# An out projection that keeps its weights standing, ten pair additions, a new order of steps, and VectorE filling a PSUM bank itself

## The chip, the cores and the metric

The kernel runs as one program on one core of a Trainium2 chip. The metric is the device time of one execution in microseconds, the median of several runs. TensorE multiplies, VectorE and ScalarE do elementwise work and can reach PSUM, GpSimd (POOL) does elementwise work in SBUF only, and SyncE (SP) issues most of the DMAs. Each engine goes through its own queue in order and waits on semaphores.

## What is computed

For 32 sequences of 128 tokens with 128 features each, in fp32:

```python
h = adapter_with_layernorm(x, language_ids)          # per-sequence weights
for layer in range(4):                               # mamba blocks
    xz = layer_norm(h) @ Wi.T;  xs, z = split(xz)
    u = silu(causal_conv4(xs) + cb)                  # 256 channels
    dt, B, C = split(u @ Wx.T);  dt = softplus(dt @ Wdt.T + bdt)
    # for each of 16 states: s = exp(dt*A)*s + dt*B*u ;  y += s*C
    y = (y + u*Dp) * silu(z)
    h = h + y @ Wo.T
x = x + h
x = x + sparse_moe(dense_moe(x))                     # dense: 8 experts and a shared one
```

The recurrence over tokens is done with one scan instruction for each pair of states.

## The kernel before

After a setup phase (the adapter) comes the **wave phase** (`wave_phase`), then a dense phase and a sparse phase for the experts. The change is in the wave phase alone.

The wave phase has NIT = 32 iterations; an iteration is one layer of one group of G = 4 sequences (512 tokens, TOK). The groups are taken in two rounds of four. An iteration `i` has NSTEP = 16 steps `k`: steps 0 to 7 are the eight pairs of states of the first 128 channels (c = 0), steps 8 to 15 those of the second 128 (c = 1). What each step does for a pair of states:

- ScalarE `decay`: dA = exp(dt * A), two activations of 128x508 (L717). Four buffers, so ScalarE can be at most four steps ahead of the scans.
- VectorE `input_term`: dB = dtu * B into PSUM, 128x1024 (L800), with dtu = dt * u standing in a PSUM bank psT. Then `scan_step`, the scan hh of dA and dB, 128x1024 (L811).
- GpSimd `weigh_states`: gg = hh * C, 128x1024 (L886). From iteration FIRST = 15 on, in the steps of PAIRED, it also adds the two halves (L890), so that TensorE has one matmul to do and not two.
- TensorE `sum_states`: adds gg into the bank psY by matmuls with the identity (L554). `skip(i, c)` (L547) opens psY for each half c with u * Dp; it has to wait until ScalarE has emptied psY (`copy_sums`, L698; in the table of ScalarE's order "sums0" and "sums1").

Beside these steps stands the work of the next iteration's projections. It all goes through one PSUM bank, psW: transposes of the normed input ("T"), then x0, x1 (4 matmuls each with the convolution's taps in the weights), z0, z1, bcdt, dt0, dt1, and "out", the out projection of the iteration before. TensorE fills psW and signals `wready`, ScalarE empties it and signals `wfree`; `psw_uses` numbers the uses in TensorE's order. At which step each engine does what is written out by hand: `PE_AT`, `ACT_AT`, `POOL_AT`. ScalarE's `silu` stands in its step 8 with two loads of its function table around it; from iteration 16 on, it also does the silu of nine gate tiles (L737) there.

In iterations under RING0 = 13 psT has two banks, one for each half of the channels, and GpSimd makes three of the 16 input products (`GIVEN`; ScalarE copies them to PSUM, L708). From iteration 13 on only psT[0] is left for dtu, because psT[1] becomes psD; ScalarE fills psT[0] twice in an iteration ("turn0", "turn1", L692), and VectorE waits for it before steps 0 and 8. dB then has one buffer, too.

From FIRST = 15 on, the dense FFN of the first round's groups is woven in: 9 gate matmuls (L580), 9 up (L588) and 9 down (L595) in each iteration, at steps given by `G_AT`, `U_AT`, `D_AT` (numbers count on past 16 into the next iteration). ScalarE copies a gate tile out five steps after its matmul (L730), VectorE multiplies it by the up matmul's result two steps after that (L831).

In TensorE's queue a step stands in this order:

```python
if k == NK: skip(i, 1)
if k > 0: sum_states(i, k)
# down, up, transpose_x, gate: as the streams say
# PE_AT's work of this step
if k == 0:
    skip(i, 0); sum_states(i, k)
```

SyncE's queue has, in the order of steps, the rows of B and C spread to 128 partitions (512 KB for each of B and C and pair), the weights of the iteration after next (`weights`, five DMAs, at k = 11, after waiting for dt1 and for `skip`), and the FFN's loads.

Of the kernel before, what the change touches and what calls it, by code (L numbers as in the profile page):

```python
# [9 lines left out]
G = 4  # L10
# [3 lines left out]
NIT = NL * NG  # L14
# [254 lines left out]
def psw_uses():  # L269

    order = [("T", 0)] + [(what, 0) for k in sorted(PE_AT) for what in PE_AT[k] if what in PRE] + [("T", 1)]
    for i in range(NIT):
        for k in sorted(PE_AT):
            for what in PE_AT[k]:
                if what in PRE and i + 1 < NIT:
                    order.append((what, i + 1))
                if what == "out" and i > 0:
                    order.append(("out", i - 1))
                if what == "transposes" and i + 2 < NIT:
                    order.append(("T", i + 2))  # L280
    order.append(("out", NIT - 1))
    return {use: n for n, use in enumerate(order)}
# [38 lines left out]
def wave_phase(nc, A, K, M, out):  # L321

    ctx = ExitStack()
    with ctx:
# [51 lines left out]
        names = ("wcur_ld wready wfree dbu da scan prod half red stat moments rs1 rs2 rstd_ok centred skipped par_ok kept_ok exp_ok ln_ok dt_ok dtu_ok placed silu_ok "  # L376
                 "ycopied ygated gave moved cleared zero zeroed x_ld x1_ok x_st gated gfree sg_ok scaled upped acted downed sum_ok").split()
        (wcur_ld, wready, wfree, dbu, da, scan, prod, half, red, stat, moments, rs1, rs2, rstd_ok, centred, skipped, par_ok, kept_ok, exp_ok, ln_ok, dt_ok, dtu_ok, placed, silu_ok,
# [50 lines left out]
        with nc.Block() as block:  # L429
            @block.sync  # L430
            def _(sp):
# [63 lines left out]
                for i in range(NIT):  # L495
                    for k in range(NSTEP):
# [4 lines left out]
                        if k == 11 and i + 2 < NIT:  # L501
                            weights(i + 2)
# [14 lines left out]
            def _(pe):  # L517
# [78 lines left out]

                transposes(0)
                for k in sorted(PE_AT):
                    for what in PE_AT[k]:
                        if what in PRE:  # L600
                            pre(0, what)
                transposes(1)
                for i in range(NIT):
                    for k in range(NSTEP):
                        if k == NK:
                            skip(i, 1)
                        if k > 0:
# [9 lines left out]
                        for what in PE_AT.get(k, ()):  # L617
                            if what in PRE and i + 1 < NIT:
                                pre(i + 1, what)
                            if what == "out" and i > 0:  # L620
                                out_projection(i - 1)
                            if what == "transposes" and i + 2 < NIT:
                                transposes(i + 2)
                        if k == 0:
                            skip(i, 0)
                            sum_states(i, k)
                out_projection(NIT - 1)

            @block.scalar
            def _(act):  # L630
# [55 lines left out]
                def place_dtu(t, c):  # L686
                    act.wait_ge(dtu_ok, t + 1)
                    if t < RING0:
                        at_least(act, scan, NSTEP * (t - 1) + NK * (c + 1))
                    else:  # L690
                        act.wait_ge(dbu, made(NSTEP * t + NK * c))
                    act.activation((psT[c] if t < RING0 else psT[0])[:, :], dtu[:, c, :], ACT.Copy).then_inc(placed, 1)  # L692

                def copy_sums(i, c):
# [3 lines left out]
                    act.activation(yg[i % 2][:, c, :], psY[:, :], ACT.Copy).then_inc(ycopied, 1)  # L698

# [45 lines left out]
                for k in sorted(ACT_AT):  # L745
                    for what in ACT_AT[k]:
                        pre(0, what)
                centre(1)
                place_dtu(0, 0)
                for i in range(NIT):  # L750
                    for k in range(NSTEP):
                        if k > 0 and assisted(i, k - 1):
                            move_given(i, k - 1)
                        for n in stream([a + 5 for a in G_AT], i, k):
# [3 lines left out]
                        if k == 12 and i > FIRST and (i - FIRST) % NF == 0:  # L758
                            place_sum((i - FIRST) // NF - 1)
                        for what in ACT_AT.get(k, ()):  # L760
                            if i + 1 < NIT:
                                pre(i + 1, what)
                            if what == "centre" and i + 2 < NIT:
                                centre(i + 2)
                            if what == "added" and i > 0:
# [9 lines left out]
                            if what == "turn0" and i >= RING0:  # L775
                                place_dtu(i, 0)
                            if what == "turn1" and i >= RING0:
# [743 lines left out]
```

## Time and profile before

| what | value |
|---|---|
| median of 3 runs | 2886.13 us (2884.73 to 2886.28) |
| the profiled execution | 2885.38 us |
| its span, first to last instruction | 2883.6 us |
| TensorE busy | 2454.6 us (85%) |
| VectorE busy | 2060.6 us (71%) |
| GpSimd busy | 2007.4 us (70%) |
| ScalarE busy | 1547.3 us (54%) |
| mean granted TensorE clock | 0.926 of full speed |

An fp32 matmul shows in the profile as two MATMUL instructions (two passes), each with a weight load. Their shown durations overlap, so a busy TensorE isn't one at its peak; the distance of their starts tells the pace. Shares are means over stages that have different limits: in the second half of the wave phase every engine has the FFN's work beside its own.

### The profile page before, as it was taken

What the parts mean: (1) busy time and instruction counts of PE and PEld (TensorE: products, weight loads), DVE (VectorE), ACT (ScalarE), POOL (GpSimd) and SP (SyncE); (2) the same over time, 40 slices, a digit from 0 to 9 for tenths busy, and PEclk for the clock granted to TensorE, in tenths of its full rate; (3) what the DMA queues carried; (4) which work ended last, traced back from release to release, by engine and by line L of the source; (5) the groups of instructions that cost most, each with busy time, mean ns of one, the idle gap of its engine ahead of it and who ended that gap; (6) DMA issues with size and microseconds to landing.
All of it is one profiled execution on the core that took longest, in us unless ns stands there. A gap on an engine that the chain in (4) does not pass through costs nothing. (4 is left out here: it accounts for less than half of the span.)

```text
span 2883.6 us, 23236 instructions
## 1 busy us (share of the span) xinstructions
PE 2454.6 (85%) x6258; PEld 1087.5 (38%) x6258; DVE 2060.6 (71%) x2022; ACT 1547.3 (54%) x2398; POOL 2007.4 (70%) x1234
## 2 busy tenths in 40 slices
PE   5488898998998888888888888988888699999586
PEld 3133333433333333333333333333333244444364
DVE  4389999999999887777777787787778633333221
ACT  2367767767766655565556565555665233232132
POOL 3389999999997877777777777777777622222176
PEclk9799998998899989999999999999999799999798
DMA  7345645644646666555555655666555330000154
GB/s 207 142 144 188 231 158 170 226 165 139 203 157 220 213 210 217 181 187 186 185 198 200 202 176 206 206 213 209 187 185 176 130 104 15 31 15 9 38 113 72
DMA packets 217995, 462.39 MB, mean 160 GB/s; under 512 B 29644, under 2 KB 111506, under 8 KB 217746
## 3 DMA queue, kind: packets, MB, share of 16 engines
q1 hardware_dynamic: 204178, 449.66, 46.9%
q0 software_dynamic: 11264, 7.98, 1.8%
q10 hardware_dynamic: 2432, 3.38, 0.3%
q8 instruction: 45, 0.74, 0.1%
q14 instruction: 76, 0.62, 0.1%
HBM read 437.51 MB, written 23.99 MB: 160 GB/s over the span
## 5 line engine op out<-in xcount | busy, mean ns | idle before, releaser
L811 DVE TENSOR_TENSOR_SCAN hh<-dA,psdB 128x1024 f32<-128x1024 f32 x512 | 1168.0, 2285 | 79.8 <-ACT dA L717 19.9
L886 POOL TENSOR_TENSOR gg<-hh,Clo 128x1024 f32<-128x1024 f32 x408 | 960.5, 2356 | 373.3 <-DVE hh L811 368.1
L554 PE MATMUL psY<-gg,ident 128*128 128x512 f32 x1776 | 922.7, 648 | 82.3 <-POOL gg L890 43.7
L717 ACT ACTIVATE dA<-dt,Acur 128x508 f32<-128x508 f32 x1024 | 668.1, 708 | 21.3 <-DVE hh L811 20.4
L800 DVE TENSOR_TENSOR psdB<-psT,Blo 128x1024 f32<-128x1024 f32 x395 | 483.2, 1223 | 112.5 <-ACT psT L692 99.5
L554 PEld LDWEIGHTS psY<-gg,ident 128*128 128x128 f32 x1776 | 341.0, 202 | 581.7 <-issue 381.2
L1276 DVE TENSOR_TENSOR ac<-sg,d_bank 128x512 f32<-128x512 f32 x144 | 99.1, 688 | 242.9 <-PE d_bank L1126 189.9
L730 ACT ACTIVATE late<-psdB 128x512 f32<-128x512 f32 x144 | 86.0, 597 | 312.2 <-PE psdB L580 312.2
L535 PE MATMUL psW<-xnT,wcur 128*128 128x512 f32 x512 | 234.7, 600 | 20.6 <-DMA diag<-diags_l 18.8
L886 POOL TENSOR_TENSOR gg<-hh,late 128x1024 f32<-128x1024 f32 x104 | 243.7, 2359 | 12.1 <-PE psY L554 8.4
L1175 ACT ACTIVATE sg<-d_bank 128x512 f32<-128x512 f32 x144 | 86.0, 597 | 261.0 <-PE d_bank L1122 255.0
L1030 POOL TENSOR_TENSOR xw<-x1T,wbc 128x512 f32<-128x512 f32 x36 | 37.5, 1044 | 255.1 <-PE d_bank L1126 243.0
L831 DVE TENSOR_TENSOR late<-late,psdB 128x512 f32<-128x512 f32 x144 | 96.5, 670 | 165.0 <-PE psdB L588 165.0
L542 PE MATMUL psW<-xd,wdcur 8*128 8x512 f32 x128 | 98.9, 862 | 100.3 <-ACT xd L673 57.0
L890 POOL TENSOR_TENSOR gg<-gg 128x512 f32<-128x512 f32 x136 | 172.2, 1266 | 10.7
L580 PE MATMUL psdB<-h_res,fw 128*128 128x512 f32 x288 | 157.2, 629 | 0.0
L588 PE MATMUL psdB<-late,fw 128*128 128x512 f32 x288 | 153.5, 615 | 0.0
L535 PEld LDWEIGHTS psW<-xnT,wcur 128*128 128x128 f32 x512 | 97.8, 192 | 146.7 <-issue 123.2
L547 PE MATMUL psY<-u,diag 128*128 128x512 f32 x128 | 86.9, 767 | 75.6 <-ACT yg L698 75.6
L1122 PE MATMUL d_bank<-x1T,wgu 128*128 128x512 f32 x288 | 148.5, 597 | 0.7 <-ACT x1T L1153 0.7
L1126 PE MATMUL d_bank<-xw,wgu 128*128 128x512 f32 x288 | 147.6, 594 | 0.0
L1349 POOL DMA_INDIRECT out<-eos,home x64 | 99.6, 1556 | 67.5 <-DVE eos L1441 46.1
(168 smaller groups left out, 2953.1 us busy)
## 6 DMA issues: line engine op xcount, KB each, us to landing
Blo<-rows SPq DMA_DIRECT2D x280, 512.0 KB, 5.3
Clo<-rows SPq DMA_DIRECT2D x280, 512.0 KB, 4.8
late<-rows SPq DMA_DIRECT2D x104, 512.0 KB, 6.4
wcur<-taps_l SPq DMA_DIRECT2D x32, 512.0 KB
disp<-fw SPq DMA_DIRECT2D x16, 528.0 KB, 8.1
dx<-disp SPq DMA_DIRECT2D x16, 528.0 KB
fw<-in_Wg SPq DMA_DIRECT2D x32, 256.0 KB, 5.0
fw<-in_Wu SPq DMA_DIRECT2D x32, 256.0 KB, 4.6
```

Of the source, the lines that this page charges most:

```text
L535: ins = pe.matmul(psW[:, :], lhsT=wcur[:, k, c * 128:(c + 1) * 128], rhs=xnT[:, :, k:k + T], start=(k == 0), stop=(k == NTAP - 1))
L554: ins = pe.matmul(psY[:, :], lhsT=ident[:, :], rhs=gg[k % NGB][:, j, :], start=False, stop=(k % NK == NK - 1 and j == last - 1))
L580: pe.matmul(psG, lhsT=fwg[:, e % NXW, f * 128:(f + 1) * 128], rhs=flat(n // NST), start=True, stop=True).then_inc(gated, 1)
L588: pe.matmul(psU, lhsT=fwu[:, e % NXW, f * 128:(f + 1) * 128], rhs=xw[:, e % NXW, :], start=True, stop=True).then_inc(upped, 1)
L717: ins = act.activation(dA[k % NDA][:, j, :, 1:T], dt[i % 2][:, c, :, 1:T], ACT.Exp, scale=Acur[i % 2][:, s:s + 1])
L800: dve.tensor_tensor(dB[b][:, :, :], (psT[c] if i < RING0 else psT[0])[:, :].unsqueeze(1).broadcast_to([128, 2, TOK]), tile(Blo, Bhi, slot( ...
L811: dve.tensor_tensor_scan(out=hh[k % NHB][:, :, :].rearrange("p c t -> p (c t)"), data0=dA[k % NDA][:, :, :, :].rearrange("p c q t -> p (c ...
L886: ins = pool.tensor_tensor(gg[k % NGB][:, :, :], hh[k % NHB][:, :, :], tile(Clo, Chi, slot(i, s)), ALU.mult)
L890: ins = pool.tensor_tensor(gg[k % NGB][:, 0, :], gg[k % NGB][:, 0, :], gg[k % NGB][:, 1, :], ALU.add)
L1122: pe.matmul(psG[r % 2][:, :], lhsT=wgu[:, e, 0, f * 128:(f + 1) * 128], rhs=x1T[p][:, :, :], start=True, stop=True).then_inc(gated, 1)
L1126: pe.matmul(psU[r % 2][:, :], lhsT=wgu[:, e, 1, f * 128:(f + 1) * 128], rhs=xw[(NE1 * h + e) % NXW][:, :, :], start=True, stop=True).then_ ...
L1349: pool.indirect_dma_start(tokens, bass.IndirectOffsetOnAxis(ap=home[p][:, n:n + 1], axis=0), eos[p][:, n, :], None, bounds_check=NSEQ * T ...
```

## The change

Four things are edited, all in `wave_phase` and its tables.

- **Out projection.** Before, one matmul with the identity brought the residual into psW, and for each of 4 sequences and 2 halves a narrow matmul (128 columns) followed with yg as the stationary operand. Now `project` ("outT") does two wide matmuls with the weights `wo` as the stationary operand, which gives the transposed result; ScalarE copies it to SBUF over yg (`place_delta`); `turn_back` ("out") adds the residual and turns the four pieces back with four narrow matmuls against the identity.
- **Pair additions.** PAIRED has ten steps and not eight (7 and 9 are new).
- **Order.** New steps for nearly all work of TensorE and ScalarE; x0 is computed two iterations ahead; in all steps but 7, 14 and 15 TensorE's `sum_states` stands last; ScalarE's sums0 comes before dt1 and softplus; gates, ups, products and downs of the FFN have new steps; SyncE's `weights` is at k = 10.
- **dtu.** From iteration 13 on VectorE itself copies dtu into psT[0] at steps 0 and 8, waits for its own copy (`turned`), and goes on. GpSimd's `time_input` waits on `turned` where it waited on `placed`.

```diff
+AHEAD = {"x0": 2, "x1": 1, "z0": 1, "z1": 1, "bcdt": 1, "dt0": 1, "dt1": 1, "outT": -1, "out": -1, "T": 2}
-PE_AT = {0: ["x0"], 1: ["x1"], 2: ["z0", "z1"], 5: ["bcdt"], 6: ["dt0", "dt1"], 8: ["out"], 13: ["transposes"]}
-ACT_AT = {1: ["params", "dtu1"], 2: ["turn0", "norm"], 3: ["sums1"], 5: ["x0"], 6: ["x1"], 7: ["z0", "z1"], 8: ["silu"], 10: ["turn1", "bcdt"], 11: ["dt0", "dt1"],
-          12: ["softplus", "sums0"], 13: ["centre"], 14: ["added"], 15: ["dtu0"]}
+PE_AT = {0: ["x1"], 1: ["z0"], 2: ["z1"], 4: ["bcdt"], 6: ["dt0"], 7: ["dt1"], 8: ["outT"], 9: ["out"], 12: ["T"], 14: ["x0"]}
+SUM_FIRST = (7, 14, 15)
+ACT_AT = {1: ["params", "dtu1", "norm"], 4: ["sums1", "x0"], 5: ["x1"], 6: ["z0"], 7: ["z1", "silu"], 10: ["bcdt"], 11: ["dt0"],
+          12: ["sums0", "dt1", "softplus"], 13: ["outT"], 14: ["added"], 15: ["centre", "dtu0"]}
-G_AT = [-9, -8, -6, -5, -4, -3, -2, -1, 3]
-U_AT = [6, 8, 9, 11, 12, 14, 15, 19, 20]
-D_AT = [10, 10, 11, 13, 14, 18, 18, 21, 22]
-T_AT = 5
-PAIRED = [0, 1, 2, 5, 8, 13, 14, 15]
+G_AT = [-8, -7, -6, -5, -4, -3, -2, 0, 1]
+C_AT = [-3, -2, -1, 0, 1, 2, 3, 5, 6]
+U_AT = [5, 7, 9, 10, 12, 13, 15, 17, 19]
+V_AT = [7, 9, 10, 12, 13, 15, 17, 19, 21]
+D_AT = [9, 9, 10, 12, 13, 15, 17, 19, 21]
+T_AT = 4
+P_SUM = 11
+PAIRED = [0, 1, 2, 5, 7, 8, 9, 13, 14, 15]
...
-                        if k == 11 and i + 2 < NIT:
+                        if k == 10 and i + 2 < NIT:
                             weights(i + 2)
...
-                def out_projection(t):
+                def project(t):
                     pe.wait_ge(ygated, NH * (t + 1))
+                    pe.wait_ge(wfree, W["outT", t])
+                    for c in range(NH):
+                        ins = pe.matmul(psW[:, :], lhsT=wo[:, layer(t) * NH + c, :], rhs=yg[t % 2][:, c, :], start=(c == 0), stop=(c == NH - 1))
+                    ins.then_inc(wready, 1)
+
+                def turn_back(t):
                     pe.wait_ge(wfree, W["out", t])
                     pe.matmul(psW[:, :], lhsT=ident[:, :], rhs=flat(group(t)), start=True, stop=False)
                     for q in range(G):
-                        for c in range(NH):
-                            ins = pe.matmul(psW[:, q * T:(q + 1) * T], lhsT=yg[t % 2][:, c, q * T:(q + 1) * T], rhs=wo[:, layer(t) * NH + c, :], start=False, stop=(q == G - 1 and c == NH - 1))
+                        ins = pe.matmul(psW[:, q * T:(q + 1) * T], lhsT=yg[t % 2][:, 0, q * T:(q + 1) * T], rhs=ident[:, :], start=False, stop=(q == G - 1))
                     ins.then_inc(wready, 1)
...
                 transposes(1)
+                pre(1, "x0")
                 for i in range(NIT):
                     for k in range(NSTEP):
-                        if k == NK:
-                            skip(i, 1)
-                        if k > 0:
+                        if k in SUM_FIRST:
                             sum_states(i, k)
...
+                        work(i, k)
+                        if k % NK == 0:
+                            skip(i, k // NK)
+                        if k not in SUM_FIRST:
                             sum_states(i, k)
-                out_projection(NIT - 1)
+                project(NIT - 1)
+                turn_back(NIT - 1)
...
+                def place_delta(t):
+                    act.wait_ge(wready, W["outT", t] + 1)
+                    act.activation(yg[t % 2][:, 0, :], psW[:, :], ACT.Copy).then_inc(wfree, 1)
...
                 def input_term(i, k):
                     n, c, s = NSTEP * i + k, k // NK, pair(i, k)
-                    if k % NK == 0:
+                    if k % NK == 0 and i < RING0:
                         dve.wait_ge(placed, NH * i + c + 1)
+                    if k % NK == 0 and i >= RING0:
+                        dve.wait_ge(dtu_ok, i + 1)
+                        dve.wait_ge(dbu, made(n))
+                        dve.tensor_copy(psT[0][:, :], dtu[:, c, :]).then_inc(turned, 1)
+                        dve.wait_ge(turned, NH * (i - RING0) + c + 1)
```

(`work` calls the functions that PE_AT names for the step, for iteration i + AHEAD.)

## Rows read from the trace of the kernel before

**Rows 1.** Busy time by stretch: us, PE, PEld, DVE, ACT, POOL, PEclk, DMA

```profile
189.20:851.70 662.50, 592.91 (x1419) 246.94 (x1418) 625.53 (x456) 478.07 (x746) 633.86 (x326) 0.93 0.54 179
851.70:911.90 60.20, 50.26 (x122) 20.16 (x120) 57.34 (x41) 39.06 (x62) 47.04 (x25) 0.97 0.58 206
911.90:975.20 63.30, 55.21 (x136) 24.05 (x137) 57.38 (x42) 40.37 (x66) 48.41 (x26) 0.95 0.72 249
975.20:2226.70 1251.50, 1087.27 (x2477) 451.31 (x2476) 991.48 (x787) 735.08 (x1106) 937.22 (x546) 0.92 0.58 194
2226.70:2286.00 59.30, 39.74 (x86) 15.28 (x84) 56.98 (x35) 19.89 (x32) 48.70 (x26) 0.88 0.47 167
```

**Rows 2.** Timeline of VectorE, iteration 25: start, us, instruction

```profile
1760.15 2.29 DVE L811 TENSOR_TENSOR_SCAN hh<-dA,psdB 128x1024 f32<-128x1024 f32 x1
1762.35 0.66 DVE L831 TENSOR_TENSOR late<-late,psdB 128x512 f32<-128x512 f32 x1
...
1764.24 2.29 DVE L811 TENSOR_TENSOR_SCAN hh<-dA,psdB 128x1024 f32<-128x1024 f32 x1
...
1768.34 2.29 DVE L811 TENSOR_TENSOR_SCAN hh<-dA,psdB 128x1024 f32<-128x1024 f32 x1
...
1772.06 2.29 DVE L811 TENSOR_TENSOR_SCAN hh<-dA,psdB 128x1024 f32<-128x1024 f32 x1
...
1838.93 2.29 DVE L811 TENSOR_TENSOR_SCAN hh<-dA,psdB 128x1024 f32<-128x1024 f32 x1
```

**Rows 3.** Waits of VectorE, 189 to 851 us: us in total, times, longest

```profile
DVE hh L811 <- ACT psdB L708: 16.4, 12, 1.4
```

**Rows 4.** Waits of VectorE, 1052 to 2152 us

```profile
DVE late L831 <- PE psdB L588: 148.3, 42, 8.0
DVE psdB L800 <- ACT psT L692: 52.6, 17, 4.0
```

**Rows 5.** Waits of all engines, iteration 25 (1760 to 1839 us)

```profile
POOL gg L886 <- DVE hh L811: 18.9, 9, 7.0
DVE late L831 <- PE psdB L588: 10.9, 3, 7.6
...
DVE psdB L800 <- ACT psT L692: 3.6, 1, 3.6
PE psY L547 <- ACT yg L698: 3.2, 1, 3.2
...
PE psW L542 <- ACT xd L673: 2.0, 1, 2.0
```

**Rows 6.** Timeline of ScalarE, iteration 25

```profile
1787.83 4.12 ACT L737 ACTIVATE late<-late 128x3072 f32<-128x3072 f32 x2
...
1793.26 2.55 ACT L717 ACTIVATE dA<-dt,Acur 128x508 f32<-128x508 f32 x4
1795.72 0.57 ACT L692 ACTIVATE psT<-dtu 128x512 f32<-128x512 f32 x1
...
1810.09 0.58 ACT L698 ACTIVATE yg<-psY 128x512 f32<-128x512 f32 x1
```

**Rows 7.** Busy time by stretch, inside iteration 25 (columns as rows 1)

```profile
1796.00:1814.00 18.00, 12.58 (x14) 4.31 (x15) 11.05 (x7) 10.06 (x16) 10.81 (x6) 0.62 0.56 179
1814.00:1838.00 24.00, 22.61 (x68) 10.96 (x67) 20.16 (x15) 12.81 (x25) 16.73 (x10) 1.00 0.63 203
```

**Rows 8.** Groups of GpSimd's instructions, iteration 25

```profile
L890 POOL TENSOR_TENSOR gg<-gg 128x512 f32<-128x512 f32 x8 | 10.1, 1267 | 0.6
```

**Rows 9.** Timeline of TensorE around the out projection, iteration 25

```profile
1815.87 1.02 PE L560 MATMUL psW<-h_res,ident 128*128 128x512 f32 x2
1816.73 1.95 PE L563 MATMUL psW<-wo,yg 128*128 128x128 f32 x16
1818.52 1.45 PE L554 MATMUL psY<-gg,ident 128*128 128x512 f32 x3
```

**Rows 10.** DMA issues of SyncE, iteration 25

```profile
1814.60 0.33 SPq L442 DMA_DIRECT2D diag<-diags_l  x1
```

More of the change, by code:

```diff
@@ L269, in psw_uses @@
 def psw_uses():
-    order = [("T", 0)] + [(what, 0) for k in sorted(PE_AT) for what in PE_AT[k] if what in PRE] + [("T", 1)]
+    order = [("T", 0)] + [(what, 0) for what in PRE] + [("T", 1), ("x0", 1)]
     for i in range(NIT):
@@ L274, in psw_uses @@
             for what in PE_AT[k]:
[L275 to L281, printed above, removed]
+                t = i + AHEAD[what]
+                if 0 <= t < NIT:
+                    order.append((what, t))
+    order += [("outT", NIT - 1), ("out", NIT - 1)]
     return {use: n for n, use in enumerate(order)}
@@ L374, in wave_phase @@
         psW = ps("psW", [128, TOK])
-        names = ("wcur_ld wready wfree dbu da scan prod half red stat moments rs1 rs2 rstd_ok centred skipped par_ok kept_ok exp_ok ln_ok dt_ok dtu_ok placed silu_ok "
+        names = ("wcur_ld wready wfree dbu da scan prod half red stat moments rs1 rs2 rstd_ok centred skipped par_ok kept_ok exp_ok ln_ok dt_ok dtu_ok placed turned silu_ok "
                  "ycopied ygated gave moved cleared zero zeroed x_ld x1_ok x_st gated gfree sg_ok scaled upped acted downed sum_ok").split()
-        (wcur_ld, wready, wfree, dbu, da, scan, prod, half, red, stat, moments, rs1, rs2, rstd_ok, centred, skipped, par_ok, kept_ok, exp_ok, ln_ok, dt_ok, dtu_ok, placed, silu_ok,
+        (wcur_ld, wready, wfree, dbu, da, scan, prod, half, red, stat, moments, rs1, rs2, rstd_ok, centred, skipped, par_ok, kept_ok, exp_ok, ln_ok, dt_ok, dtu_ok, placed, turned, silu_ok,
          ycopied, ygated, gave, moved, cleared, zero, zeroed, x_ld, x1_ok, x_st, gated, gfree, sg_ok, scaled, upped, acted, downed, sum_ok) = (sem(n) for n in names)
@@ L595, in down, with work @@
                     pe.matmul(psD[:, :], lhsT=fwd[:, e % NXW, f, :], rhs=sg[:, n % NSLG, :], start=(n % NST == 0), stop=(n % NST == NST - 1)).then_inc(downed, 1)
+                def work(i, k):
+                    for what in PE_AT.get(k, ()):
+                        t = i + AHEAD[what]
+                        if not 0 <= t < NIT:
+                            continue
+                        if what in PRE:
+                            pre(t, what)
+                        if what == "outT":
+                            project(t)
+                        if what == "out":
+                            turn_back(t)
+                        if what == "T":
+                            transposes(t)
                 transposes(0)
[L598 to L601, printed above, removed]
+                for what in PRE:
+                    pre(0, what)
                 transposes(1)
+                pre(1, "x0")
                 for i in range(NIT):
                     for k in range(NSTEP):
-                        if k == NK:
-                            skip(i, 1)
-                        if k > 0:
+                        if k in SUM_FIRST:
                             sum_states(i, k)
@@ L687, in place_dtu @@
                     act.wait_ge(dtu_ok, t + 1)
[L688 to L692, printed above, removed]
+                    at_least(act, scan, NSTEP * (t - 1) + NK * (c + 1))
+                    act.activation(psT[c][:, :], dtu[:, c, :], ACT.Copy).then_inc(placed, 1)
                 def copy_sums(i, c):
@@ L744, in _ @@
                 centre(0)
-                for k in sorted(ACT_AT):
-                    for what in ACT_AT[k]:
-                        pre(0, what)
+                for what in ("params", "norm", "x0", "x1", "z0", "z1", "silu", "bcdt", "dt0", "dt1", "softplus"):
+                    pre(0, what)
                 centre(1)
@@ L753, in _ @@
                             move_given(i, k - 1)
-                        for n in stream([a + 5 for a in G_AT], i, k):
+                        for n in stream(C_AT, i, k):
                             place_gate(n)
@@ L757, in _ @@
                             place_x((i - FIRST + 1) // NF)
-                        if k == 12 and i > FIRST and (i - FIRST) % NF == 0:
+                        if k == P_SUM and i > FIRST and (i - FIRST) % NF == 0:
                             place_sum((i - FIRST) // NF - 1)
@@ L764, in _ @@
                                 centre(i + 2)
+                            if what == "outT" and i > 0:
+                                place_delta(i - 1)
                             if what == "added" and i > 0:
@@ L774, in _ @@
                                 place_dtu(i + 1, 0)
-                            if what == "turn0" and i >= RING0:
-                                place_dtu(i, 0)
-                            if what == "turn1" and i >= RING0:
-                                place_dtu(i, 1)
                         decay(i, k)
@@ L781, in _ @@
                 copy_sums(NIT - 1, 1)
+                place_delta(NIT - 1)
                 added(NIT - 1)
@@ L840, in _ @@
                         scan_step(i, k)
-                        for n in stream([a + 2 for a in U_AT], i, k):
+                        for n in stream(V_AT, i, k):
                             act_product(n)
```

12 lines of the change are left out of this document (2 added, 10 removed).

## The prediction

> **What bounds the kernel now.** I call one pass of the wave phase's outer loop an iteration (i = 0 to 31) and its 16 inner steps k = 0 to 15. A scan (L811) is the first instruction that surely stands once in each step, so an iteration runs from the start of its k = 0 scan to the next one's.
>
> I read the table of stretches first [rows 1], cut at such scans. The reader is to see that the twelve iterations 1 to 12 take 662.5 us, 55.2 each, and the sixteen iterations 15 to 30 take 1251.5 us, 78.2 each; iteration 25 taken alone, 1760.15 to 1838.93, is 78.8 [rows 2]. In the first half VectorE is busy 625.5 of 662.5, in the second 991.5 of 1251.5, while TensorE is busy 1087.3 and GpSimd 937.2: nobody is full. So the second half is bound by a chain that goes round between engines, and the first half by VectorE.
>
> Then VectorE's waits. In the first half they are small (the largest 16.4 us, for a product that ScalarE copies in) [rows 3]. In 14 iterations of the second half VectorE waits 148.3 us for the FFN's up matmul (L588) and 52.6 us for ScalarE's copy of dtu into PSUM (L692) [rows 4]: 14.4 us an iteration. In iteration 25 they are 10.9 and 3.6, 14.5 together [rows 5]. Without them it would have lasted 78.8 - 14.5 = 64.3 us.
>
> Where do they come from? ScalarE's order, read off its timeline [rows 6]: the silu block with two table loads ends in 4.12 us of gate silus at 1787.83, and only after it and two decays comes the dtu copy at 1795.72. That is the 3.6. `sums0` (L698, which empties psY) comes at 1810.09, behind dt0, dt1 and softplus; TensorE's `skip(i,1)` waits 3.2 us for it, and the up matmul that VectorE wants is behind that skip: the 7.6. TensorE also waits 2.0 for xd. [...] This whole knot, k = 6 to 10, is what the change re-orders.
>
> **The change part by part, for one second-half iteration.**
>
> *VectorE copies dtu.* It adds 2 copies of 128x512. No row has this copy; the nearest are the product L831 of the same shape, 0.66 us, and what an extra one costs in the queue: the step with it takes 1764.24 - 1760.15 = 4.09, one without it 1772.06 - 1768.34 = 3.72, so 0.37 [rows 2]. The copy is followed by a wait for its own end (`turned`), which the plain product isn't. Bounds 0.37 and 0.8 (0.66 and a gap of 0.1) each; I take 0.55, between them, as the wait is real: +1.1 us on VectorE. It takes the 3.6 us wait away. What is late next there is decay(8), the first two of the four activations at 1793.26, so about 1794.5; but the silu block also moves one step forward (k = 8 to 7, with z1), since z0, z1 and the last two gates come a step or two sooner, so I take nothing for it. The copies need only dtu_ok, whose POOL product (k = 11 before) is over 4 steps early. ScalarE loses two copies of 0.57 and gains one (`place_delta`).
>
> VectorE's floor is then 64.3 + 1.1 = 65.4.
>
> *Ten pair additions.* Steps 7 and 9 join PAIRED. GpSimd: 2 x 1.27 = 2.5 us, and 2 gaps of 0.1 [rows 8]. It idles 18.9 us of iteration 25 waiting for scans [rows 5], so its floor goes from 78.8 - 18.9 = 59.9 to 62.6, still under 65.4. If VectorE's floor were the lower one this would be the bound. TensorE saves 2 matmuls of 0.86 (1816.73 - 1815.87 is one, two passes) [rows 9]: -1.7.
>
> *Out projection.* Before, one wide matmul and 16 narrow passes, 0.86 + (1818.52 - 1816.73) = 2.65 us [rows 9]. After: `project` 2 wide, `turn_back` 1 wide and 8 narrow passes, 3 x 0.86 + 0.9 = 3.5. So +0.8 us, no saving; weight loads go from 9 to 7 pairs but the row shows 112 ns a narrow pass, a quarter of a wide one, so they were hidden. TensorE in all -0.9. [...] It is also a new hop, TensorE to ScalarE to TensorE, `outT` at 8, copy at ScalarE's 13, `out` at 9.
>
> *New order.* In most steps the state sum now comes last, so up, gate and projections no longer wait for POOL's product of the same step. z0/z1 and dt0/dt1 are split over two steps with work between, so that psW's single bank is emptied meanwhile. sums0 comes before dt1 and softplus. I follow the knot, from the iteration's start, at the floor's pace: scan 7 ends at 30.6; product and pair addition are done at 34.8; then TensorE has state sum 7, up(7), dt1, gate(8), 0.7 us of wait for dt1's two copies, outT (2), skip, state sum 8, down (2), up(9): 11 matmuls of 0.86, 9.4 + 0.7, so 45.0. VectorE wants that up after scan 10, which ends at 43.1. A stall of 2 us is left of 7.6, at full clock. Ahead of it TensorE still idles about 3 us before dt0 (xd comes after the silu block and three decays, at about 29.4, TensorE is free at 26.2) and 2.8 before state sum 7. So I expect the clock still to fall for a part of the knot, some 8 passes at 0.43: +3.5. The other two smaller stalls (10.9 - 7.6 = 3.3) go, as their ups stand ahead of the sums.
>
> L = 65.4 + 2 + 3.5 = 70.9; I take 70.8 us.
>
> *Moved waits.* T goes to 12 and x0 to 14, two iterations ahead; x0's weights are issued in iteration 25 up to 1814.60 [rows 10], right after the skip, 5 DMAs that now stand before the spreads of step 11 instead of after. x0 at step 14 is over 15 us later: covered. The queue behind that wait on SP are spreads half an iteration early. If x0 had to wait, state sum 15, up and gate would be behind it.
>
> **The sum**, against the profiled run's own 2885.4 us (span 2883.6 and 1.8 around it; the median is 2886.1, 0.7 above). Iterations 15 to 30: 16 x 70.8 - 2 (30 is short, it has no gates) = 1130.8, for 1251.5: -120.7. Iterations 13 and 31 (60.2 and 59.3 now) show no stall worth the name, so the copies cost +1.1 each; 14 (63.3) goes to its floor of about 61.8: -1.5. Iterations 1 to 12: the new order takes some of the 22 us of waits (16.4 the largest), but GpSimd is busy 633.9 of 662.5 [rows 1, 3]: between 0 and -8, I take -4. Iteration 0: x1 of the next pass now stands before the first skip and sum, 4 matmuls, +3. The last out projection is exposed: 0.8 and a copy, +1.7. The dense and sparse phases, 2883.6 - 2286.0 = 597.6 us, don't change. Together -120.7 + 1.1 + 1.1 - 1.5 - 4 + 3 + 1.7 = -119.3: 2766 us.
>
> **The rivals.**
> A (forecast), L 69 to 74: 2737 to 2817.
> [...]
> C, the stall moves elsewhere (outT's copy stands behind softplus on ScalarE, and `added` behind it; or GpSimd's now 3.7 us a step in 10 steps beside scans of 3.7 leaves it no room to catch up): L about 76, 2849 us.
> D, slower: x0 at step 14 comes before its input is there. norm stands on ScalarE in the next iteration's step 1, behind three gate copies that each wait for TensorE. It has about 5 us of slack (6.9 us of TensorE work from T to x0, less 2 for T and norm). Each microsecond beyond is one per iteration, with sums and ups behind it; from 7.5 us beyond the slack (119.3 / 16) the gain is gone, and with 9.2 L = 80, 2913 us. Against: norm follows T within 2 us now.
> E, no change within 0.2% (what a measurement of this kernel can tell): C or D of just the size.
>
> Chances: A 0.58, B 0.17, C 0.18, D 0.04, E 0.03. Range: A alone 2737 to 2817; with most of B and the near part of C 2715 to 2832. Faster by over 0.2%: 0.93; within: 0.03; slower: 0.04.
>
> **What would show it.** VectorE's wait for psT's copy gone and a copy of about 0.6 us at k = 0 and 8; its wait for L588's successor 2 to 6 us an iteration, all of it after scan 10; psY's skip not waiting for ScalarE; TensorE's clock in the knot above 0.62; iterations 15 to 30 at 71 us, 1 to 12 at 55. Wrong if VectorE waits for anything new (decays, scans), if GpSimd stops waiting for scans in the second half, or if iterations 1 to 12 get longer.

## The result and the profile after

The changed kernel takes 2795.2 us (median, 2792.5 to 2798.5) where the kernel before takes 2886.2: ratio 0.9684, 95% interval 0.9667 to 0.9701, 91 us or 3.2% faster. The forecast was 2766 us, range 2715 to 2832.

The table of stretches of the changed kernel, cut at the k = 0 scans of iterations 1, 13, 14, 15, 31 and the end of 31, then two stretches inside iteration 25 (columns as in [rows 1]):

```profile
187.50:854.30 666.80, 599.77 (x1372) 247.26 (x1370) 626.08 (x457) 488.82 (x761) 634.39 (x325) 0.95 0.51 178
854.30:915.50 61.20, 53.79 (x117) 21.65 (x118) 58.50 (x43) 36.96 (x58) 48.08 (x26) 0.92 0.59 198
915.50:976.70 61.20, 55.19 (x135) 22.77 (x134) 58.50 (x43) 39.11 (x63) 47.40 (x26) 1.00 0.74 252
976.70:2132.90 1156.20, 1026.28 (x2351) 427.62 (x2349) 1015.08 (x820) 728.36 (x1091) 977.99 (x579) 0.96 0.63 211
2132.90:2193.80 60.90, 38.93 (x75) 15.37 (x74) 57.18 (x35) 18.82 (x30) 50.61 (x28) 0.84 0.46 160
1720.00:1730.00 10.00, 7.04 (x16) 2.52 (x15) 8.53 (x7) 9.97 (x13) 7.04 (x7) 1.00 0.03 7
1730.00:1748.00 18.00, 17.61 (x43) 7.54 (x42) 14.22 (x10) 11.77 (x19) 14.47 (x9) 0.91 0.62 213
```

Against [rows 1] the reader is to see one stretch that moved: iterations 15 to 30 went from 1251.5 to 1156.2 us, 78.2 to 72.3 each. Iterations 1 to 12 got 4.3 us longer, 13 got 1.0 longer, 14 got 2.1 shorter, 31 got 1.6 longer. In the knot of iteration 25 (steps 6 to 10) TensorE's granted clock is 0.91, where the stretch of the same length before had 0.62 [rows 7]. Iteration 25 is one of the short ones, though, at 70.7 us. Cut in the same way, 34 to 52 us after each iteration's start, the knots of iterations 15 to 30 have clocks from 0.72 to 1.00, mean 0.90 (before: 0.59 to 0.76, mean 0.70), and the five with the lowest, 0.72 to 0.82, belong to iterations of 72.8 to 75.0 us.

The waits of VectorE, then of TensorE, in iterations 15 to 30 of the changed kernel (us in total, times, longest):

```profile
DVE late L849 <- PE psdB L595: 91.0, 43, 6.2
DVE hh L829 <- ACT dA L732: 14.3, 11, 3.6
```

```profile
PE psW L539 <- ACT sz L676: 43.2, 16, 4.4
PE psY L556 <- POOL gg L909: 39.3, 22, 2.5
PE psW L544 <- ACT xd L687: 37.2, 16, 3.7
```

VectorE waits 5.7 us an iteration for the up matmul and not 10.6 (148.3 / 14, [rows 4]). It no longer waits for a dtu copy, but it now waits for decays in this stretch, 0.9 us an iteration. The skip (L549) waits for nobody. But at the head of TensorE's list is a wait that was small before (14.6 us): z1 (L539) waits 2.7 us an iteration for ScalarE's copy of z0. ScalarE's timeline of iteration 25 says why; two lines of TensorE's and one of GpSimd's stand below it:

```profile
1713.19 0.60 ACT L676 ACTIVATE sz<-psW 128x512 f32<-128x512 f32 x1 [2.76 <-POOL yg L892]
...
1715.01 0.60 ACT L676 ACTIVATE sz<-psW 128x512 f32<-128x512 f32 x1
1715.62 1.28 ACT L679 ACT_TABLE_LOAD   x1
...
1724.26 3.76 ACT L732 ACTIVATE dA<-dt,Acur 128x508 f32<-128x508 f32 x6
```

```profile
1709.64 1.02 PE L539 MATMUL psW<-xnT,wcur 128*128 128x512 f32 x2
...
1713.84 1.13 PE L539 MATMUL psW<-xnT,wcur 128*128 128x512 f32 x2 [2.33 <-ACT sz L676]
```

```profile
1711.84 1.26 POOL L892 TENSOR_TENSOR yg<-yg,sz 128x512 f32<-128x512 f32 x1
```

The copy of z0 overwrites the sz buffer that GpSimd's gate1 still reads (L892, its step 3: y of the second half times silu(z)). ScalarE stands idle for 2.8 us, and TensorE's z0 had ended 2.5 us before the copy began. Behind the copy stand z1, the silu block, decay(7) (the first pair at 1724.26) and xd, the copy of bcdt's result that dt0 needs.

VectorE in the same iteration, around its copy at k = 8 and around the stall:

```profile
1725.62 2.29 DVE L829 TENSOR_TENSOR_SCAN hh<-dA,psdB 128x1024 f32<-128x1024 f32 x1 [0.89 <-ACT dA L732]
1727.82 0.66 DVE L849 TENSOR_TENSOR late<-late,psdB 128x512 f32<-128x512 f32 x1
1728.40 0.69 DVE L811 COPY psT<-dtu 128x512 f32<-128x512 f32 x1
1729.12 1.23 DVE L818 TENSOR_TENSOR psdB<-psT,Blo 128x1024 f32<-128x1024 f32 x1
...
1738.18 2.29 DVE L829 TENSOR_TENSOR_SCAN hh<-dA,psdB 128x1024 f32<-128x1024 f32 x1
1743.85 0.69 DVE L849 TENSOR_TENSOR late<-late,psdB 128x512 f32<-128x512 f32 x1 [3.39 <-PE psdB L595]
```

The copy takes 0.69 us. The stall after scan 10 is 3.4 us; it was 7.6 [rows 5].

### The profile page after: what moved, and what is told of

The parts are those of the page before. It is cut to its first block and busy times, and to the rows that moved or that the text cites. A ratio compares the mean times of both kernels' runs of the same rounds, so it can differ in the third digit from the quotient of the medians.

```text
span 2792.6 us, 22910 instructions
## 1 busy us (share of the span) xinstructions
PE 2405.9 (86%) x6062; PEld 1063.7 (38%) x6062; DVE 2086.9 (75%) x2060; ACT 1547.7 (55%) x2392; POOL 2048.7 (73%) x1268
## 5 line engine op out<-in xcount | busy, mean ns | idle before, releaser
L556 PE MATMUL psY<-gg,ident 128*128 128x512 f32 x1708 | 882.7, 643 | 90.6 <-POOL gg L909 56.8
L556 PEld LDWEIGHTS psY<-gg,ident 128*128 128x128 f32 x1708 | 328.9, 202 | 553.0 <-issue 373.2
L909 POOL TENSOR_TENSOR gg<-gg 128x512 f32<-128x512 f32 x170 | 215.5, 1268 | 13.3
L849 DVE TENSOR_TENSOR late<-late,psdB 128x512 f32<-128x512 f32 x144 | 96.6, 671 | 92.9 <-PE psdB L595 92.4
L709 ACT ACTIVATE yg<-psY 128x512 f32<-128x512 f32 x64 | 38.2, 597 | 208.9 <-PE psY L556 208.9
L602 PE MATMUL psT<-late,fw 128*128 128x512 f32 x288 | 150.7, 615 | 0.0
L587 PE MATMUL psdB<-h_res,fw 128*128 128x512 f32 x288 | 150.2, 603 | 0.0
```

The lines of the kernel that those rows point to most:

```text
L556: ins = pe.matmul(psY[:, :], lhsT=ident[:, :], rhs=gg[k % NGB][:, j, :], start=False, stop=(k % NK == NK - 1 and j == last - 1))
L587: pe.matmul(psG, lhsT=fwg[:, e % NXW, f * 128:(f + 1) * 128], rhs=flat(n // NST), start=True, stop=True).then_inc(gated, 1)
L602: pe.matmul(psD[:, :], lhsT=fwd[:, e % NXW, f, :], rhs=sg[:, n % NSLG, :], start=(n % NST == 0), stop=(n % NST == NST - 1)).then_inc(downe ...
L909: ins = pool.tensor_tensor(gg[k % NGB][:, 0, :], gg[k % NGB][:, 0, :], gg[k % NGB][:, 1, :], ALU.add)
```

## The experiments

All times are medians; the ratio is to the kernel before on the same chip. Besides the medians I give the length of iterations 15 to 30 in the profiled run, for the changed kernel 72.3 us.

**a1, a2: who copies dtu.** a1 is the kernel before with the copies on VectorE, a2 the changed kernel with the copies back on ScalarE.

```diff
 # a1: before.py                                # a2: after.py, the reverse, and
-ACT_AT = {... 2: ["turn0", "norm"], ... 10: ["turn1", "bcdt"], ...}
+ACT_AT = {... 2: ["norm"], ... 10: ["bcdt"], ...}
+                        dve.tensor_copy(psT[0][:, :], dtu[:, c, :]).then_inc(turned, 1)
```

> The kernel before, with the one edit that VectorE copies dtu into psT[0] itself from iteration 13 on. Theory 1 (a knot in TensorE's chain sets the pace): the 3.6 us wait per iteration goes, but the up matmul that VectorE wants after scan 10 comes no sooner, except for the 0.57 us that ScalarE saves ahead of xd, so the wait for it grows by about as much and the copies' 1.1 us are hidden in it too: 2870 to 2886 us, wait for L588's successor 11 to 13.5 us an iteration. Rival (waits add up): 16 x (3.6 - 1.1) = 40 us saved, 2846.

> The changed kernel, with dtu copied by ScalarE again from iteration 13 on (at ScalarE's steps 2 and 10, as in the kernel before). Theory 1: in the new order the silu block ends a step earlier, but decays 7, 8 and 9 now stand between it and the copy, so VectorE waits about 2.5 us for the copy at step 8 and saves 1.1 us of copies: part of it is hidden in the 3.8 us stall after scan 10, and xd comes 0.6 us later: 16 x 0.5 to 1.5 = 8 to 24 us slower than the changed kernel, 2803 to 2819. Rival (VectorE is the bound and the new order has removed the wait): 16 x 1.1 = 18 us faster, 2777. Second rival: the copy carries the gain, 16 x 3.6 slower, 2850.

a1: 2882.3 us, ratio 0.9990 (0.9975 to 1.0004), as theory 1 had it. a2: 2796.1 us, ratio 0.9685 (0.9656 to 0.9715), 72.3 us per iteration; the 8 to 24 us of loss that were expected didn't come. In these two pairs of kernels the copies on VectorE are worth nothing that the runs can tell. In a2 the wait of 2.5 us for the copy at step 8 isn't there: the new order has removed it without VectorE's help. VectorE's wait for ups is 109.0 us, 18 more than in the changed kernel: what it saves on its two copies it waits at the next place.

```profile
DVE psdB L820 <- ACT psT L706: 1.6, 3, 0.5
```

The waits of VectorE in iterations 15 to 30 of a1 show where the 61.8 us went that the kernel before waits for copies there:

```profile
DVE late L829 <- PE psdB L588: 192.2, 47, 10.4
DVE hh L809 <- ACT dA L714: 2.1, 2, 1.1
```

The same group in the kernel before has 165.0 us in these iterations. So of 61.8 us, 27 went into more waiting for the up matmul, 2 into decays and 16 (32 x 0.5) into the copies; 16 are left in this profiled run, which at 2874.9 us is the shortest of ten, and 4 between the medians. Most of the gain on paper turned into waiting at the next place.

**a3: the narrow out projection in the changed kernel.**

```diff
-PE_AT = {... 8: ["outT"], 9: ["out"], ...}
+PE_AT = {... 9: ["out"], ...}
-                        ins = pe.matmul(psW[...], lhsT=yg[t % 2][:, 0, q * T:(q + 1) * T], rhs=ident[:, :], ...)
+                        for c in range(NH):
+                            ins = pe.matmul(psW[...], lhsT=yg[t % 2][:, c, q * T:(q + 1) * T], rhs=wo[:, layer(t) * NH + c, :], ...)
```

> The changed kernel with the old out projection (one wide and 16 narrow passes, at step 9; project, place_delta and the step outT are gone). Theory 1: two wide matmuls (1.7 us) and the wait for dt1's copies (0.4) leave the chain from state sum 7 to up(9), 0.8 us are put behind that up: the stall after scan 10 shrinks from 3.4 by up to 2 us, 16 x 1.5 = 24 us faster than the changed kernel, 2771. Rival (standing weights pay): 0 to 15 us slower, 2795 to 2810, with narrow passes above 0.13 us.

2765.4 us, ratio 0.9583 (0.9559 to 0.9607): 30 us faster than the changed kernel, 70.4 us per iteration, and VectorE's wait for ups 63.4 us where it was 91.0. The edit changes three things at once: TensorE's work at step 8 goes, with its wait of 7.3 us in 16 iterations for dt1's copies, ScalarE's copy of the result goes, and the passes are others. Together this is 1% of the kernel; no run parts it. TensorE's timeline of the changed kernel shows its own share:

```profile
1737.50 1.96 PE L563 MATMUL psW<-yg,wo 128*128 128x512 f32 x4 [0.39 <-ACT soft L692]
1739.29 1.02 PE L549 MATMUL psY<-u,diag 128*128 128x512 f32 x2
...
1744.44 1.02 PE L568 MATMUL psW<-h_res,ident 128*128 128x512 f32 x2
1745.30 1.05 PE L570 MATMUL psW<-ident,yg 128*128 128x128 f32 x8
1746.19 1.02 PE L556 MATMUL psY<-gg,ident 128*128 128x512 f32 x2
```

1.79 and 1.75 us, 3.5 in all as the prediction had it, against 2.65 [rows 9]; and the first half of it stands between dt1 and the up matmul that VectorE wants.

**a4, b1: the pair additions.** a4 is the changed kernel with the old PAIRED, b1 the kernel before with the new one.

```diff
-PAIRED = [0, 1, 2, 5, 8, 13, 14, 15]
+PAIRED = [0, 1, 2, 5, 7, 8, 9, 13, 14, 15]      # b1; a4 the reverse
```

> The changed kernel with eight pair additions (not in steps 7 and 9). Theory 1: GpSimd's product of step 7 is there 1.3 us earlier, state sum 7 takes 0.86 longer, state sum 9 stands behind the up that counts: -0.5 to +0.9 us per iteration, 2787 to 2810. Rival (GpSimd is too full): 16 x 1.3 faster, 2775. Second rival (TensorE is too full): 16 x 1.7 slower, 2822.

> The kernel before with ten pair additions (steps 7 and 9 too). Theory 1: state sum 7 stands before skip and up(8) and gets 0.86 us shorter (up to 1.7 at the low clock), its product is 1.3 us later but has been waiting there for 7 us; state sum 9 is 0.86 shorter after the knot: 0.5 to 1.5 us per iteration, 8 to 24 us faster, 2862 to 2878. Rival (GpSimd is the bound): 16 x 2.5 slower, 2926.

a4: 2799.8 us, ratio 0.9706 (0.9678 to 0.9734), which overlaps the changed kernel's interval. b1: 2857.8 us, ratio 0.9905 (0.9889 to 0.9922), 28 us faster than before, a little beyond the 8 to 24 expected. Why the same two additions count in one order and hardly in the other isn't fully shown. State sum 7 stands ahead of its up matmul in both kernels; only state sum 9 has changed its place. The waits give a part of it. In the kernel before TensorE waits no more for products with ten additions than with eight (39.3 and 41.0 us in 16 iterations). In the changed kernel it waits 41.8 us with ten and 31.0 with eight, so part of what the shorter sums save is lost there in waiting for products that come 1.3 us later.

**b2, d1: the place of the state sums.** b2 is the changed kernel with the sums first again, d1 the kernel before with this place changed.

```diff
-                        if k in SUM_FIRST:                      # (7, 14, 15)
+                        if k in (1, 2, 3, 4, 5, 6, 7, 9, 10, 11, 12, 13, 14, 15):     # b2
                             sum_states(i, k)
                         ...down, up, gate, work, skip...
```

> The changed kernel with the state sums first in every step but 0 and 8 (as in the kernel before), all other positions as changed. Theory 1: every up, gate and projection waits for GpSimd's product of its own step again, 2 to 4 us per iteration: 2827 to 2859. Rival (the place of the sums doesn't matter, the other moves do): within 5 us of the changed kernel.

> The kernel before with only the place of the state sums changed as in the changed kernel (last in every step but 7, 14 and 15; skip(i, 1) right before the sum of step 8), all tables as before; a second, identical copy of the last FFN sum at the end is left out. The changed kernel with the sums first lost 119 us, so theory 3 says that the place of the sums is the main gain: ups and gates stand one product sooner: 60 to 100 us faster than before, 2786 to 2826. Rival (place and tables need each other: here skip still waits for sums0 behind softplus and the double copies of psW stay): 0 to 40 us faster, 2846 to 2886.

Two things go with it in d1: skip(i, 1), which opens psY for the second half, moves from the head of step 8 to right before its state sum, and a second copy of the last FFN sum, after the last iteration, is left out. In b2 the skip keeps its new place.

b2: 2914.5 us, ratio 1.0105 (1.0088 to 1.0122), 119 us slower than the changed kernel, far beyond the 2827 to 2859 expected, and slower than before: without the sums' place all the rest of the change together is a loss. d1: 2802.6 us, ratio 0.9718 (0.9698 to 0.9738), 84 us faster than before with the old tables. TensorE's waits in iterations 15 to 30, b2 first:

```profile
PE psY L556 <- POOL gg L909: 91.1, 40, 5.3
PE psY L556 <- POOL gg L905: 57.4, 32, 3.6
```

And d1:

```profile
PE psW L542 <- ACT xd L672: 51.9, 16, 5.6
PE psW L537 <- ACT sz L661: 34.5, 16, 2.8
PE psW L542 <- ACT soft L677: 21.7, 16, 1.4
PE psY L554 <- POOL gg L888: 2.9, 2, 2.5
```

In b2 TensorE waits 148.5 us for products, 41.8 in the changed kernel, and each of these waits stands in front of ups and gates. The kernel before waits 41.0 us for products and 50.9 us at skip for sums0; in d1 these are 2.9 us and nothing, with sums0 still behind softplus: the work of step 8 now stands ahead of the skip. How much of the 84 us is the skip's new place and how much that of the sums no run parts in the old tables; b2, where the skip stays late, shows that the sums count by themselves in the new ones. VectorE's waits in d1, then one of ScalarE's:

```profile
DVE late L829 <- PE psdB L588: 82.0, 43, 2.8
DVE psdB L798 <- ACT psT L691: 68.3, 31, 5.4
```

```profile
ACT sz L661 <- POOL yg L871: 46.5, 16, 3.7
```

The wait for ups is half of the 165 us it was; the one for ScalarE's copies is about what it was (61.8). And z0's wait for gate1, 9.8 us in the kernel before, is 46.5 us here, with every step of the tables where it was: the new place of the sums is enough to bring that wait.

**b3: sums0 behind softplus in the changed kernel.**

```diff
-          12: ["sums0", "dt1", "softplus"],
+          12: ["dt1", "softplus", "sums0"],
```

> The changed kernel with ScalarE's sums0 behind dt1 and softplus in its step 12, as in the kernel before. Theory 1: skip(i, 1) waits for it: dt1's two copies and the softplus pair, 3.4 us, all on the chain to up(9), less 1.3 of outT's wait that overlaps: 2.5 to 3.5 us per second-half iteration, 40 to 56 us slower, 2835 to 2851. Rival (skip has slack): within 8 us.

2805.2 us, ratio 0.9732 (0.9711 to 0.9752): 10 us slower than the changed kernel, 14 by the ratios, not 40 to 56. TensorE's skip waits 9.3 us in 16 iterations for it. I had counted too little for outT, whose 1.8 us stand between dt1's copies and the skip: in iteration 25 of the changed kernel ScalarE's softplus ends at 1739.5 and TensorE's skip starts at 1739.29, so sums0 behind the softplus is late by little more than its own 0.6 us.

**b4: gate1 one step earlier.**

```diff
-POOL_AT = {3: ["gate1"], ...}
+POOL_AT = {2: ["gate1"], ...}
```

> The changed kernel with GpSimd's gate1 in step 2 and not 3. The trace of the changed kernel shows a wait that the prediction hadn't: ScalarE's copy of z0 waits 50 us in 16 iterations for gate1 (sz is reused), which makes z1, the silu block, decay(7) and xd late. Theory 2: gate1 comes 3.7 us sooner, z0 waits 0 to 0.5, decay(7) is in time (19.5 us of waits in iterations 1 to 12, 14 in the second half), xd 3 us sooner: 8 to 12 us in the first half and 1 to 2 per iteration in the second, 2755 to 2772. Rival (the late silu is hidden; the stall is set by GpSimd's product of step 7): 0 to 8 us faster, 2787 to 2795.

2760.5 us, ratio 0.9562 (0.9546 to 0.9578): 35 us faster than the changed kernel, 70.2 us per iteration. VectorE's waits in iterations 15 to 30, then TensorE's for the copy of z0:

```profile
DVE late L849 <- PE psdB L595: 71.2, 27, 6.2
DVE hh L829 <- ACT dA L732: 0.8, 2, 0.5
```

```profile
PE psW L539 <- ACT sz L676: 3.2, 5, 1.0
```

43.2 became 3.2, the decays' 14.3 became 0.8, the ups' 91.0 became 71.2. For the second half the theory holds. For iterations 1 to 12 it fell: they take 663.8 us, 3.0 less and not 8 to 12, and VectorE still waits 19.2 us for decays there.

**c1, c2: the two gains together, and x0 behind the sum.** c1 is b4 with a3; c2 is c1 with this:

```diff
-PE_AT = {... 12: ["T"], 14: ["x0"]}
+PE_AT = {... 12: ["T"], 15: ["x0"]}
```

> The changed kernel with both: gate1 in GpSimd's step 2 and the old narrow out projection at step 9. Each alone gave about 30 and 35 us over the changed kernel (70.4 and 70.2 us per second-half iteration where it has 72.3). Theory 2 (the two waits lie on one chain to the up after scan 10, one ahead of state sum 7, one behind it): the gains add up as long as a stall is left: 68.5 per iteration, 2730 to 2738. Rival (either is enough, what is left is hidden behind GpSimd's product of step 7 or VectorE's floor of 65.4): 2750 to 2760.

> As c1, and x0 in TensorE's step 15, behind its state sum, and not in step 14 ahead of it. In iterations 1 to 12 VectorE waits 20 us for decay(7) and decay(12); the trace has ScalarE waiting 4.8 us for the last state sum, which stands behind x0's four matmuls (3.4 us), and the silu block and decay(7) late behind that. Theory: sums1 3.4 us sooner, decay(7) in time, 6 to 12 us faster than c1 in the first half; x1 now follows x0 with only a gate between, and waits some 1 us for x0's copy on ScalarE: in all 2720 to 2732. Rival (x0's copy comes later by as much as sums1 comes sooner): within 4 us of c1.

c1: 2732.2 us, ratio 0.9464 (0.9451 to 0.9476), 68.2 us per iteration: the gains add up, and this is the fastest version, 63 us under the changed kernel. VectorE's wait for ups is 41.3 us:

```profile
DVE late L838 <- PE psdB L590: 41.3, 32, 2.2
```

c2: 2753.9 us, ratio 0.9541 (0.9528 to 0.9554), 22 us slower than c1. The first half didn't move (666.2 us, 25.6 us of waits for decays), so that theory fell. The loss is in iterations 15 to 30, 25 us; there ScalarE waits 104.6 us for x0 and x1 in psW where c1 has 44.6. That x0 and x1 now stand nearly back to back is the likely cause, but it wasn't tested.

**d3: all but the tables.** The kernel before with d1's place of the sums, ten pairs, VectorE's copies and gate1 in step 2.

```diff
-                        if k == NK:
-                            skip(i, 1)
-                        if k > 0:
+                        if k in (7, 14, 15):
                             sum_states(i, k)
 ...
-POOL_AT = {3: ["gate1"], ...}
+POOL_AT = {2: ["gate1"], ...}
 # and PAIRED as b1, the copies as a1; PE_AT, ACT_AT, G_AT, U_AT, D_AT, out projection as before
```

> The kernel before with the sums last (as d1), ten pair additions, VectorE's copies of dtu and gate1 in GpSimd's step 2; all steps of TensorE and ScalarE, the FFN's positions, x0's lead and the narrow out projection as before. It stands beside c1 (2732 us), from which only those tables tell it apart. Theory 3 (the place of the sums is nearly all, the tables little): 2735 to 2760. Rival (the tables' step by step order counts once the sums are last: z0 and z1 back to back, dt0 and dt1 back to back, sums0 behind softplus): 2765 to 2795.

2740.9 us, ratio 0.9516 (0.9503 to 0.9529), 69.3 us per iteration. Beside the other changes, all that the new steps of TensorE and ScalarE, the FFN's new positions and x0's lead are worth is the distance to c1, ratio 0.0052, some 15 us (8.7 between the medians, on two chips). In the profiled runs it has two parts: c1 is 17 us shorter in iterations 15 to 30 (1091.2 and 1108.4) and 7 us longer in 1 to 12 (666.2 and 659.3). VectorE's waits in iterations 15 to 30 of d3:

```profile
DVE late L827 <- PE psdB L588: 66.9, 32, 3.6
```

d3 is 62 us faster than d1 (58 by the ratios). Three edits stand between them, the pair additions, VectorE's copies and gate1's step, and no run parts them. In d1 VectorE waits 68.3 us for ScalarE's copies, in d3 for none, so that the copies may well be worth something in that order, though a1 and a2 found nothing in theirs.

## Why the prediction was right or wrong

**The direction and the place were right.** All of the gain is in iterations 15 to 30 (95.3 us there, with small changes of both signs elsewhere), and it came out of VectorE's wait for the up matmul and the copy.

**VectorE's floor** was forecast at 65.4 us: iteration 25 takes 70.7, of which 3.8 are waits for ups, 0.9 for a decay and 0.4 others, so 65.6; the sixteen iterations less such waits give 65.7. Right. The copies were booked at 0.55 each. In iteration 13, where a copy stands right behind a scan and VectorE waits for nobody, two of them took the iteration from 60.2 to 61.2, so 0.5. In the FFN's iterations nearly all of them stand behind a gate product (L849), and there the step with product and copy takes 4.82 us (1725.62 to 1730.44) where the step with the product alone takes 4.09 [rows 2]: 0.73 each, 0.4 us an iteration more than booked.

**The copies' worth.** The prediction booked the removed 3.6 us straight into the floor. a1 shows that in the kernel before most of it goes into the next wait, and a2 that in the new order ScalarE's copies cost nothing either. That the sum came out even so is luck: the wait did go, but by the new order, not by VectorE's copies.

**The out projection** was sized right (3.5 us, no gain) and put in the right place, in the chain to the up: a3 got back 30 us. These fp32 passes start 430 ns apart at 512 columns (1744.44 to 1745.30 above, two passes) and 112 at 128 (1745.30 to 1746.19, eight), as in [rows 9]. In a3 the 16 narrow passes take 1.78 us up to the start of the next matmul (iteration 24, 1662.61 to 1664.39), so 0.11 each, and not the over 0.13 that its rival asked for.

**The pair additions** were booked as 1.7 us of TensorE's and hardly used in the sum. In the new order they are worth little (a4, within the error); in the old one they gave 28 us.

**New order: the step that failed.** I made the knot, with sums0 before dt1 and softplus on ScalarE, the main thing, and the sums' new place one sentence of four. It is the other way round: sums0's place is worth 10 to 14 us (b3), the sums' place, with the skip's, 84 in the old tables, and the sums' alone 119 inside the changed kernel (d1, b2). The tables themselves are worth some 9 to 15 us beside the other changes (d3 against c1).

**The size: a wait overlooked.** L was forecast at 70.8 us and measured at 72.3; iteration 30, forecast at 68.8, took 74.8. In all iterations 15 to 30 are 25.4 us longer than forecast, iterations 1 to 12 are 8.3 longer and iteration 0 is 6.3 shorter, and the difference to 2766 is 28 us in the profiled run (29 in the medians). The prediction let ScalarE empty z0 as soon as TensorE had it. The copy also waits for `ygated`, GpSimd's gate1 in its step 3: TensorE waits 2.7 us an iteration for that, and it is worth 35 us (b4). z0 moved one step forward while gate1 stayed, but d1 has the same wait with both in their old steps, so it is the sums' place that brought it out.

The waits beyond VectorE's floor were forecast as 2 us of stall and 3.5 for a low clock, 5.5 in all, and measured as 5.7 for ups and 0.9 for decays, 6.6. In b4, without the wait for gate1, they are 4.5 and L is 70.2. So two errors of opposite sign met: a wait of 2.1 us an iteration that wasn't in the sum, and an allowance for the rest that was 1 us too large. That L came within 1.5 us is in part luck. The 3.5 us for the clock were eight passes at 0.43 each. No run shows this term as a whole: both the number of passes and that the clock falls because TensorE idles were my estimates. What the traces show is the cost of one slow pass: in iteration 25 of the kernel before three passes take 2.56 us at a granted clock of 0.50 (1803.25 to 1805.81), 0.85 each, where a pass takes 0.43 at 1.00, so 0.42 more; and, in the changed kernel's iteration 25, four such passes and 1.8 us, as shown below. The clock did fall in the knot. A stretch inside that of iteration 25 (columns as in [rows 1]) and the lines of TensorE around it:

```profile
1731.00:1733.00 2.00, 2.00 (x3) 0.64 (x3) 1.97 (x2) 1.19 (x2) 1.87 (x3) 0.50 0.01 4
```

```profile
1729.60 4.54 PE L556 MATMUL psY<-gg,ident 128*128 128x512 f32 x6
1733.98 1.02 PE L595 MATMUL psdB<-late,fw 128*128 128x512 f32 x2
```

State sums 6 and 7 of iteration 25, right ahead of the up, take 4.4 us for six passes (the profile has no wait among them), where six at a clock of 1.00 take 2.6 (430 ns each): 1.8 us, against the 3.5 that I had allowed. The last four of them, 1730.67 to 1733.98, take 3.31 us and not 1.72. In iteration 26 the same six take 5.3 us, so 2.7.

**The first half**, forecast -4, came out +4.3, with 19.5 us of waits for decays (6.0 before, and the waits for the given products fell from 16.4 to 7.4). b4, c1 and c2 keep these waits; d1 and d3, with the old tables, have 0.4 and 3.2, and their iterations 1 to 12 take 655.9 and 659.3 us where the kernel before takes 662.5. So it is the tables that cause them; which entry was not settled. Silu in ScalarE's step 7, ahead of decay(7), is the likely one, but that is only argued.

**Iteration 0** went the other way too, 64.3 us for 67.6, where I had put +3; the reason wasn't looked for.

**The signs of being wrong.** Of the three that the prediction named, two came: VectorE waits for something new, the decays, and iterations 1 to 12 got longer. The third didn't: GpSimd still waits 157.1 us for scans in iterations 15 to 30. And VectorE's wait for ups isn't all after scan 10: it falls in 43 pieces over 16 iterations, though in iteration 25 the stall after scan 10 is 3.4 of 3.8 us. The direction and the place were right, but these two signs say that the account of the new order was incomplete, as the runs then showed.

**The rivals.** B (the knot dissolves and the clock stays high, 68 us, 2721 in all) has the length of c1 (68.2), but c1's granted clock in iterations 15 to 30 is 0.96, no higher than the changed kernel's 0.96. C (76 us) was half right in kind: a wait grew elsewhere, but at gate1 and by less. D (x0 too early) didn't occur: TensorE waits 0.4 us for x0's and x1's bank in sixteen iterations. c2, with x0 later, was slower.

## What to carry to other kernels

Where an engine's queue is written by hand, first ask in which order the items of one step stand: what needs another engine's fresh product goes last, behind everything that others are waiting for. That edit was worth 84 us here, and the long tables around it some 9 to 15.

A removed wait is worth only what the next wait on the same chain lets through; follow the chain to where both paths join before booking it. And when a producer comes sooner, by its own move or by another's, list all that its consumer's copy waits for, the release of its destination too: the reader of the old contents (here gate1) has to move with it.

The form with fewer weight loads gained nothing here, where a narrow pass with a weight load of its own takes 112 ns, about a quarter of a wide one's 430 [rows 9], and its detour over another engine made the chain it stands in longer.

## What the runs showed of the hardware

VectorE copies 128x512 fp32 from SBUF to PSUM in 0.67 us (a1, 32 copies, mean 673 ns) to 0.69 us (the changed kernel, 32 copies, mean 685 ns). In the changed kernel such a copy with a wait for its own end adds 0.5 us to VectorE's queue right behind a scan (iteration 13, two copies: 61.2 us for 60.2) and 0.73 behind a 128x512 product (the step from 1725.62 to 1730.44: 4.82 us for 4.09).

At a granted clock of 1.00 two fp32 passes of TensorE with 512 columns start 430 ns apart, and with 128 columns 112 ns ([rows 9], in a stretch of 1.00 by [rows 7]; 1744.44 to 1746.19 in the changed kernel). At 0.50 passes with 512 columns start 0.85 us apart (before, 1803.25 to 1805.81, three passes). A matmul of two such passes so takes 1.7 us and not 0.86. The passes come with one weight load each: 2477 and 2476 in iterations 15 to 30 before [rows 1]. A wide pass is shown as 592 ns long (L560, both passes in iteration 25 before) and the next starts 430 ns after it, so the shown durations overlap by 162 ns. In 1731 to 1733 of the changed kernel TensorE is shown busy for 2.00 of 2.00 us at a granted clock of 0.50, with pass starts 0.85 us apart (1731.53 and 1732.38).

No instruction of GpSimd in the trace of the kernel before reads or writes a PSUM bank; VectorE (L800, psdB) and ScalarE (L692, psT) write them.

In these runs the mean granted clock doesn't tell which version is faster: 0.946 in the profiled run of the changed kernel (2795 us), 0.946 in c1's (2732 us), 0.940 in d3's (2741 us).
